# The stretch between two graph layers as a pipeline over chunks of node blocks, with two terms formed during layer 0

## What is computed

```python
h = relu(layernorm(x))
# layer 0: degree-normalised sum over the edges
deg  = segment_sum(1, dst) + 1;  dis = rsqrt(deg)
hw   = h @ W
agg  = segment_sum(hw[src] * (dis[src] * dis[dst])[:, None], dst)
out  = agg + hw * (dis * dis)[:, None] + b
x    = x + (h + gelu(out, approximate=False))
h = relu(layernorm(x))
# layer 1: a message network per edge, an update network per node
m    = relu(concat(h[src], h[dst], edge) @ msg_W1 + msg_b1) @ msg_W2 + msg_b2
agg  = segment_sum(m, dst)
x    = x + relu(concat(agg, h) @ upd_W1 + upd_b1) @ upd_W2 + upd_b2
```

## Time and profile before

| | us |
|---|---|
| median of three timed runs | 2646.51 |
| lowest and highest of them | 2634.43, 2647.69 |
| the profiled execution | 2642.74 |
| its span in the trace | 2641.0 |
| layer 0's sums | about 190 to 820 |
| stretch between the layers, up to the first split copy | 820 to 886 |
| split, clearing and pass setup | 886 to 912 |
| message pass | 912 to 2578 |
| update network | 2578 to the end |

### The profile page before, as it was taken

How to read it: one execution, slowest core, us unless ns; L and a number is a source line. 1 busy time by engine, 2 the same in 40 slices (tenths; PEclk the granted TensorE clock), 3 DMA queues, 4 the chain that set the end, 5 groups by cost and what they waited for, 6 DMA issues and landing times.

```text
span 2641.0 us, 71244 instructions
## 1 busy us (share of the span) xinstructions
PE 2303.5 (87%) x22534; PEld 1988.5 (75%) x22535; DVE 1827.3 (69%) x5068; ACT 1130.6 (43%) x2326; POOL 1829.3 (69%) x1684
## 2 busy tenths in 40 slices
PE   2357999999994499999999999999999999999988
PEld 1246778777873378888888888888888888888874
DVE  8876777777786676666666666666666666666642
ACT  0016778878883133333333333333333333333321
POOL 2647777777770067777777777777777777777770
PEclk7569999999997699999999999999999999999986
DMA  2011111111120323333233333233223333332331
GB/s 65 1 27 27 27 28 27 28 28 28 28 28 2 71 50 64 66 65 65 63 64 65 66 65 65 65 65 65 64 63 65 66 66 66 66 65 65 64 49 24
DMA packets 349624, 134.26 MB, mean 51 GB/s; under 512 B 306107, under 2 KB 323361, under 8 KB 349473
## 3 DMA queue, kind: packets, MB, share of 16 engines
q1 hardware_dynamic: 297506, 79.11, 13.3%
q0 software_dynamic: 51968, 53.32, 10.8%
HBM read 124.78 MB, written 7.49 MB: 50 GB/s over the span
## 4 chain that ended last, share of the span: by engine, by line
PE 34%; POOL 32%; issue 13%; DVE 10%; DMA 6%; SPq 3%; ACT 1%; DVEq 1%; POOLq 0%; PEldq 0%; ACTq 0%
POOL rows L573 32%; PE psum L1306 8%; PE psum L1337 6%; PE psum L1458 4%; PE psum L1423 3%; DMA rows<-a_rows,idx 3%; PE psum L1432 2%; DMA idx<-src_by_tile 2%; PE psum L1470 2%; PE psum L1443 2%; PE psum L1327 2%; DVE H L949 1%; SPq L445 1%; PE psum L1414 1%; PE psum L1515 1%
## 5 line engine op out<-in xcount | busy, mean ns | idle before, releaser
L573 POOL DMA_INDIRECT rows<-a_rows,idx x1176 | 1284.1, 1092 | 496.0 <-issue 337.7
L573 POOL DMA_INDIRECT rows<-g_rows,idx x448 | 463.1, 1034 | 169.4 <-issue 135.0
L1115 ACT ACTIVATE hT<-psum 128x392 bf16<-128x392 f32 x1120 | 496.7, 502 | 139.2 <-PE psum L1337 131.8
L949 DVE TENSOR_SCALAR H<-Y,node_cmp 128x512 bf16<-128x512 f16 (+1 forms) x1372 | 383.0, 353 | 192.8 <-ACT Y L1150 192.8
L1458 PE MATMUL psum<-edge_index,H 128*128 128x192 bf16 x4802 | 430.3, 247 | 32.0 <-DVE H L949 32.0
L1306 PE MATMUL psum<-work,hT 128*128 128x192 bf16 x3430 | 447.1, 248 | 0.3 <-ACT hT L1115 0.3
L1458 PEld LDWEIGHTS psum<-edge_index,H 128*128 128x128 bf16 x4802 | 397.1, 99 | 54.9 <-issue 52.2
L1337 PE MATMUL psum<-Z,one_lo 128*128 128x392 f16 x1120 | 359.3, 342 | 28.8 <-DVE Z L827 28.6
L1423 PE MATMUL psum<-wb,eoT 128*128 128x64 f32 x3136 | 380.3, 275 | 0.0
L1306 PEld LDWEIGHTS psum<-work,hT 128*128 128x128 bf16 x3430 | 317.7, 99 | 70.6 <-issue 3.5
L1423 PEld LDWEIGHTS psum<-wb,eoT 128*128 128x128 f32 x3136 | 368.9, 193 | 0.1
(11 more groups left out here) (237 smaller groups left out, 2140.3 us busy)
## 6 DMA issues: line engine op xcount, KB each, us to landing
work<-in_edge_attr_dram SPq DMA_DIRECT2D x390, 128.0 KB
rows<-a_rows,idx POOLq DMA_INDIRECT x1176
Z<-slot_code SPq DMA_DIRECT2D x98, 128.0 KB, 3.0
rows<-g_rows,idx POOLq DMA_INDIRECT x448
idx<-src_by_tile SPq DMA_DIRECT2D x203, 4.0 KB, 1.8
wb<-b_rows SPq DMA_DIRECT2D x196, 16.0 KB, 1.9
g_rows<-Y SPq DMA_DIRECT2D x1, 1600.0 KB, 7.1
a_rows<-Y SPq DMA_DIRECT2D x1, 1600.0 KB, 7.2
```

The source lines that it names most:

```text
L573: pool.indirect_dma_start(out=rows[:, k, t, :], out_offset=None, in_=table, in_offset=bass.IndirectOffsetOnAxis(ap=idx[:, k, t:t + 1], axis=0)
L949: ins = V.tensor_scalar(pick[:, b, cols], slot_src[:, cols], node_cmp[:, b:b + 1], None, ALU.is_equal)
L1115: nc.scalar.activation(counts[:, j % 2, :, t * SLOTS:(t + 1) * SLOTS], psum[:, t % 4, 0:KEYS].rearrange("p (h m) -> p h m", m=SLOTS), ACT.Copy
```

## The change

Seven chunks of eight blocks (`NCHUNK`; the last has two) take the place of the whole-array operations in the stretch.

- In `mixed_step` of body 0, at the head of steps 2 to 8, VectorE runs `own_terms`: for each block of one chunk `Y * dis + b_l0` in place (the scale is one value for each partition), and then `X + H` for that chunk. It waits for the weights and for the store of `g_rows` first.
- In the stretch VectorE runs `scale_sums` (one instruction for each block: PSUM times `dis` plus `Y`), `centre` (add GELU's output, sum, mean, subtract) and `variance`, each one chunk later than the one ahead of it. ScalarE runs GELU and the squares by chunk. The square root is one instruction still. TensorE's transposes of `acc` use four banks.
- The normalise, TensorE's transposes of `H` (banks 0, 1, 6, 7) and products, and the copies run by chunk. ScalarE copies the transposed blocks to `hT` and the products' first half to `Y`, VectorE forms the second half, and SP stores each chunk of both as soon as it is there.

```diff
+            def own_terms(c):
+                if c == 0:
+                    dve.wait_ge(s_wt, 11 * 16)
+                    dve.wait_ge(s_gd, 16)
+                m = min(T, NB - c * T)
+                for b in range(c * T, c * T + m):
+                    V.scalar_tensor_tensor(Y[:, b, :], Y[:, b, :], dis[:, b:b + 1], b_l0[:, :], ALU.mult, ALU.add)
+                V.tensor_tensor(X[:, c * T:c * T + m, :], X[:, c * T:c * T + m, :], H[:, c * T + 1:c * T + m + 1, :],
+                                ALU.add).then_inc(s_own, 1)
...
             def mixed_step(i, j):
                 started = not isinstance(i, int) or i * MB + j >= 2
+                if isinstance(i, int) and 2 <= j < 2 + NCHUNK:
+                    own_terms(j - 2)
...
-            for c in range(0, NB, T):
-                m = min(T, NB - c)
-                dve.wait_ge(s_stT, c // T + 1)
-                V.tensor_tensor(Z[:, c:c + m, :], psum[:, (c // T) % 2, 0:m * D].rearrange("p (b d) -> p b d", d=D),
-                                Y[:, c:c + m, :], ALU.add).then_inc(s_stc, 1)
-            link(V.tensor_tensor(X[:, :, :], X[:, :, :], H[:, 1:NB + 1, :], ALU.add))
...
-            layer_norm_relu(1)
...
+            def scale_sums(c):
+                dve.wait_ge(s_stT, c + 1)
+                for b in range(chunk(c).start, chunk(c).stop):
+                    ins = V.scalar_tensor_tensor(Z[:, b, :], psum[:, c % 4, (b % T) * D:(b % T + 1) * D], dis[:, b:b + 1],
+                                                 Y[:, b, :], ALU.mult, ALU.add)
+                ins.then_inc(s_gelu_in, 1)
+
+            def centre(c):
+                cols = chunk(c)
+                dve.wait_ge(s_gelu, c + 1)
+                link(V.tensor_tensor(X[:, cols, :], X[:, cols, :], Z[:, cols, :], ALU.add))
+                link(V.tensor_reduce(s1[:, cols], X[:, cols, :], AX, ALU.add))
+                link(V.tensor_scalar(mean[:, cols], s1[:, cols], 1.0 / D, None, ALU.mult))
+                V.tensor_tensor(Y[:, cols, :], X[:, cols, :], per_node(mean, c), ALU.subtract).then_inc(s_centred, 1)
+
+            def variance(c):
+                cols = chunk(c)
+                dve.wait_ge(s_square, c + 1)
+                V.tensor_reduce(s2[:, cols], Z[:, cols, :], AX, ALU.add).then_inc(s_var[1], 1)
+
+            for c in range(NCHUNK + 2):
+                if c < NCHUNK:
+                    scale_sums(c)
+                if 1 <= c <= NCHUNK:
+                    centre(c - 1)
+                if c >= 2:
+                    variance(c - 2)
...
+            for c in range(3):
+                normalise(c)
+            for c in range(NCHUNK):
+                if c + 3 < NCHUNK:
+                    normalise(c + 3)
+                target_rows(c)
...
-            act.wait_ge(s_gelu_in, 1)
-            nc.scalar.activation(Z[:, :, :], Z[:, :, :], ACT.Gelu).then_inc(s_gelu, 1)
-            sqrt_var(1)
...
+            for c in range(NCHUNK + 1):
+                if c < NCHUNK:
+                    act.wait_ge(s_gelu_in, c + 1)
+                    nc.scalar.activation(Z[:, chunk(c), :], Z[:, chunk(c), :], ACT.Gelu).then_inc(s_gelu, 1)
+                if c >= 1:
+                    act.wait_ge(s_centred, c)
+                    nc.scalar.activation(Z[:, chunk(c - 1), :], Y[:, chunk(c - 1), :], ACT.Square).then_inc(s_square, 1)
...
+            copy_quad(0)
+            copy_quad(1)
+            for c in range(NCHUNK):
+                for q in (2 * c + 2, 2 * c + 3):
+                    if q < NQUAD:
+                        copy_quad(q)
+                act.wait_ge(s_ab, c + 1)
...
+                nc.scalar.activation(Y[:, chunk(c), :], ps3[:, :, 0:D], ACT.Copy).then_inc(s_ac, 1)
...
+            transpose_quad(0)
+            transpose_quad(1)
+            for c in range(NCHUNK):
+                for q in (2 * c + 2, 2 * c + 3):
+                    if q < NQUAD:
+                        transpose_quad(q)
+                source_and_target_rows(c)
```

More of the change, by code:

```diff
@@ L258, in gnn_two_layers @@
         s_gd = sem("s_gd")
-        s_abd = sem("s_abd")
+        s_ad = sem("s_ad")
+        s_bd = sem("s_bd")
+        s_own = sem("s_own")
         s_stT = sem("s_stT")
@@ L263, in gnn_two_layers @@
         s_gelu = sem("s_gelu")
+        s_centred = sem("s_centred")
+        s_square = sem("s_square")
+        s_quad = sem("s_quad")
+        s_quadc = sem("s_quadc")
+        s_ab = sem("s_ab")
+        s_ac = sem("s_ac")
+        s_bc = sem("s_bc")
         s_deg = sem("s_deg")
@@ L302, in gnn_two_layers @@
         b_in = [sem(f"b_in{k}") for k in range(U)]
-        counts_reset = [sem(f"counts_reset{l}") for l in range(3)]
+        counts_reset = {l: sem(f"counts_reset{l}") for l in (1, 2)}
         s_binoh = sem("s_binoh")
@@ L424, in _ @@
             sp.dma_start(code_dram.rearrange("(a q) e -> q a e", a=4), code_rows[0:NPT // 4, :, :]).then_inc(s_coded, 16)
[L425 to L428, removed]
+            for c in range(NCHUNK):
+                m = min(T, NB - c * T)
+                for table, held, copied, stored in ((a_dram, Y, s_ac, s_ad), (b_dram, Z, s_bc, s_bd)):
+                    sp.wait_ge(copied, c + 1)
+                    sp.dma_start(table[c * T * P:(c * T + m) * P, :].rearrange("(b p) d -> p b d", p=P),
+                                 held[:, c * T:c * T + m, :]).then_inc(stored, 16)
+            sp.wait_ge(s_ad, 16 * NCHUNK)
+            sp.wait_ge(s_bd, 16 * NCHUNK)
             sp.wait_ge(s_coded, 16)
@@ L1040, in _ @@
[L1040 to L1045, removed]
-            layer_norm_relu(1)
[L1048 to L1055, removed]
+            dve.wait_ge(s_stc, 1)
+            dve.wait_ge(s_own, NCHUNK)
+            def chunk(c):
+                return slice(c * T, min(NB, c * T + T))
+            def per_node(t, c):
+                m = chunk(c).stop - chunk(c).start
+                return wide(t[:, chunk(c)].rearrange("p (b d) -> p b d", d=1), 2, D)
@@ new lines, in _, with normalise, target_rows @@
+            link(V.reciprocal(rstd[:, :], std[:, :]))
+            def normalise(c):
+                cols = chunk(c)
+                V.scalar_tensor_tensor(H[:, cols.start + 1:cols.stop + 1, :], Y[:, cols, :], 0.0, per_node(rstd, c), ALU.max, ALU.mult
+                                       ).then_inc(s_hready[1], 1)
+            def target_rows(c):
+                cols = chunk(c)
+                m = cols.stop - cols.start
+                dve.wait_ge(s_ac, c + 1)
+                j = 2 + 2 * (c % 2)
@@ L1070, in _ @@
             dve.wait_ge(s_split_a, NPART)
-            dve.wait_ge(s_abd, 32)
+            dve.wait_ge(s_ad, 16 * NCHUNK)
+            dve.wait_ge(s_bd, 16 * NCHUNK)
             message_passes()
@@ L1386, in _ @@
[L1386 to L1395, removed]
@@ L1396, in _, with transpose_quad @@
-            pe.wait_ge(s_mmc, 2 * ((NB + T - 1) // T))
+            NQUAD = -(-NB // 4)
+            def transpose_quad(q):
+                if q == 0:
+                    pe.wait_ge(s_gelu_in, NCHUNK)
+                if q >= 4:
+                    pe.wait_ge(s_quadc, q - 3)
+                pe.wait_ge(s_hready[1], q // 2 + 1)
+                for b in range(4 * q, min(NB, 4 * q + 4)):
+                    ins = TT.transpose(psum[:, QUAD_BANK[q % 4], (b % 4) * P:(b % 4 + 1) * P],
+                                       H[:, b:b + 2, :].rearrange("p b d -> p (b d)"), ident[:, :])
+                ins.then_inc(s_quad, 1)
@@ new lines, in source_and_target_rows @@
+            def source_and_target_rows(c):
+                pe.wait_ge(s_quadc, min(NQUAD, 2 * c + 2))
+                if c >= 2:
+                    pe.wait_ge(s_ac, c - 1)
+                    pe.wait_ge(s_bc, c - 1)
+                for b in range(c * T, min(NB, c * T + T)):
+                    j = 2 + 2 * (c % 2) + (b % T) // 4
+                    ins = TT.matmul(psum[:, j, (b % 4) * 2 * D:(b % 4 + 1) * 2 * D], hT[D:2 * D, b * P:(b + 1) * P],
+                                    w_ab[D:2 * D, :], start=True, stop=True)
+                ins.then_inc(s_ab, 1)
```

50 lines of the change are left out of this document (30 added, 20 removed).

## The result

The changed kernel takes 2653.99 us (median of 8 runs, 2649.27 to 2667.34), the kernel before 2641.65 (8 runs, 2634.43 to 2647.69) beside it: a ratio of 1.0051, 95% interval 1.003 to 1.0071. It is slower by half a percent where 0.5% faster was forecast, and the time lies outside the range. The profiled execution has a span of 2651.3 us, 10.3 more than before.

A forecast was written before the change was run, and what follows sets the result against it. VectorE's chain, then its TensorE ping-pong and row products, bound the stretch; GpSimd's gathers, then TensorE, bound body 0. Gains 7.3 + 6.4 less 2 make 11.7 us off 2642.74: 2631, put at 2632, range 2619 to 2644.

The forecast's parts named there:

- Part 1: Stretch between the layers up to the normalise: VectorE stays the bound, 30.3 us instead of 37.6, gain 7.3.
- The 64-wide piece: VectorE's new scale-and-add with a per-partition pointer: taken at 0.20 us each, 10.2 us for 50, ends 6.5 and 13.5.
- the 128-wide row: Profile row of a 128-wide PSUM operation on VectorE, 0.19 us: read as agreeing with 58 fixed cycles, not 120.
- A round: VectorE's work per chunk in the stretch: 4.5 us, with ScalarE's GELU and squares, some 0.6 each, beside it.
- The load in the open: ScalarE's table load ahead of the square root, earlier beside VectorE's work: 1.28 us now uncovered.
- rival 3: Square not in GELU's table on ScalarE: each turn loads 1.28 us, 1 to 2 us more, 2634; chance 0.08.
- Part 2: Normalise to last copy: TensorE starts after one chunk, four banks end the ping-pong; 20.7 us instead of 27.1, gain 6.4.
- Queues and stores: Two 1.6 MB stores become fourteen, covered by the message pass setup: nothing gained, nothing lost.
- Part 3: Own terms in steps 2 to 8 of body 0: 14 us more VectorE work, GpSimd's gathers lose 2 us.
- the dense start: Early gathers beside VectorE running without a break: 4.1 us lost in 10, a rate giving a loss up to 6.
- the cover: Steps 2 to 8: VectorE's 1.0 us of register loads and 1.95 of waiting absorb the own terms; VectorE's delay costs 0.
- Rival 4: Body 0: VectorE's own terms block GpSimd's gathers, 31 us lost on the gather path, 2660; chance 0.06.

The follow-up runs named there:

- one-wait kernel: The changed kernel plus one VectorE wait for its own terms behind each chunk of them: 2633.69 us, ratio 0.9982 to the kernel before.
- two-wait kernel: The changed kernel with a VectorE wait behind each chunk's own terms, plus a second for the step's partial sum: 2636.83 us, ratio 0.997 to the kernel before.
- that with the sums: The changed kernel with own terms moved to the stretch's head and four unused 512-wide sums replacing them in steps 2 to 8: 2660.49 us, one execution.

## Why the prediction was wrong

**Part 1 was right.** 30.3 us forecast from the first piece to the normalise, 874.90-845.16 = 29.7 measured. The 64-wide piece 0.20, measured 0.19. The Trainium skill's 120 cycles plus elements for PSUM sources ("VectorE: DVE Perf Modes", TRN2 errata) gives 0.19 too, so here its figure holds where the 128-wide row had spoken against it; by that row's 0.06 us of overhead and no pointer it would have been 0.13. What costs the difference isn't separated. The own terms L864 read SBUF alone and come every (1.65-0.27)/7 = 0.20 us, so the PSUM source isn't needed for it; the pointer or the three-operand form is left, and no run tells them apart. A round 4.5, measured 4.38. The load in the open, and none between GELU and Square: rival 3 is out.

**Part 2 was right in size.** 20.7 forecast, 21.7 measured. A chunk took 3.0 us of TensorE (882.34 to 885.34) where I had 2.7, and that is the 1 us. What I didn't see is that the clock need not rise: I read from the earlier trace rows that it does after 4 us and took that as a price. In the four profiles with the whole-array stretch the clock rose 3.0 to 3.8 us after the first transpose; in two of the eight with the pipeline it never rose in part 2, and 14.5 us went with it.

**Queues and stores** cost nothing, as forecast.

**Part 3 failed, at one term:** "The 448 gathers lost about 42 us beside 473 us of VectorE, 0.09 per us; 14 us of extra work lose 1.3, up to 6 at the rate of the dense start (4.1 us in 10). I take 2." Measured: 26.1 us in body 0. A rate per microsecond of VectorE's work is the wrong kind of price. The one-wait kernel has the same work and loses 10.7, the two-wait kernel 2.6. The price hangs on gaps. And the cover that I named just ahead of it, "VectorE's 1.0 us of register loads and 1.95 us of waiting in the step absorb it", was just these gaps: I spent as free the idle time in which GpSimd got through. VectorE's own delay was small, nearly as I had it: its one-hots of steps 2 and 3, which no late gather can have delayed yet, begin 1.0 and 1.2 us later against the first gather than before.

**Rival 4 was the case,** with a mechanism close to the right one and 31 us for 26.1; I gave it 0.06. Its argument for, that 2.2 us ahead of the keys make 5 us without a break, was right and even short (8.2 us, since the 0.26 us of waiting ahead of the step's partial sum vanished too). Its argument against, that the 2.7 us runs of steps 3 to 8 lose only 0.3 a step, was read from runs with a gap at both ends. The row that spoke clearly, 2.75 us beside ten unbroken microseconds at 189 to 200, I averaged away. The range to 2644 left it out.

The sum with the measured terms: 12.9 us gained, 23.5 lost, 10.6 in all; the profiled spans differ by 10.3.

## What to carry to other kernels

Before work is put into an engine's idle time, ask who else lives on that idleness: a neighbour may be getting through only where the engine pauses. If such a neighbour sets the pace, a wait added to the busy engine can make the kernel faster, and the place for extra work is where the neighbour has finished. Before a stage in which TensorE alone sets the time, look at the work it had just ahead and at the granted clock of several executions, not of one.

## What the runs showed of the hardware

- A gather of GpSimd (0.94 us alone) that meets VectorE's one-hots and keys without a gap takes up to 5.14 us. In the changed kernel and in that with the sums, the first held gather of a step ends 0.77 to 0.78 us after the partial sum out of PSUM (L849) begins, and the second, all but one, 0.81 to 0.82 us after VectorE's run ends. One two-input 512-wide add (L865) with a gap behind it makes it up to 1.97 us. A gap of 0.035 us, from a semaphore wait on each key instruction, lets it through (0.95 to 1.01 us each), and two-input 64-wide pieces 0.2 us apart leave it at 1.02.
- After 23 us of idling TensorE's granted clock stayed at 0.50 through some 35 us of nearly unbroken work in two profiles of eight, and rose after 3.2 to 4.9 us in six. With 6.3 to 6.7 us of bf16 matmuls ending 1.3 to 1.9 us ahead it was at 1.00 from the first transpose in all three profiles.
- The message pass has a second pace, 31.8 instead of 33.5 us for four superblocks, into which one execution fell midway, 41 us of difference in all. What tips it is open; it would be worth more than this whole change.
- One chip took 1.53 times as long for both kernels, at a mean clock of 0.782 rather than 0.935. What bounds the kernel there was not followed up, so the ratio taken there isn't set beside the others.
